# Tokens loaded with features on partitions, LayerNorm 1 applied behind the q product, low parts on GpSimd

## The reference

```
xn  = (x - mean(x)) / sqrt(var(x) + 1e-5)                 # LayerNorm 1
q   = head_norm(xn @ Wq + bq)                             # 16 heads of 32
k,v = split(y_main @ [Wk, Wv] + [bk, bv]); k = head_norm(k)
kd, vd = the same from y_dca @ Wkv_dca
x1  = x + (softmax(q k' s) v + softmax(q kd' s) vd) @ Wo + bo
out = x1 + fake_quant(relu(fake_quant(LN(x1)) @ fake_quant(F) + fake_quant(b)))
```

## Time and profile before

| | us |
|---|---|
| median of 3 runs | 370.63 |
| lowest, highest run | 370.16, 372.56 |
| profiled execution: span from the first to the last instruction | 366.4 |
| busy in the span: PE, DVE, ACT, POOL | 317.5, 315.4, 225.1, 173.5 |

### The profile page before, as it was taken

How to read it: one execution, slowest core, us unless ns; L and a number is a source line. 1 busy time by engine, 2 the same in 40 slices (tenths; PEclk the granted TensorE clock), 3 DMA queues, 4 the chain that set the end, 5 groups by cost and what they waited for, 6 DMA issues and landing times.

```text
span 366.4 us, 7583 instructions
## 1 busy us (share of the span) xinstructions
PE 317.5 (87%) x2338; PEld 255.8 (70%) x2353; DVE 315.4 (86%) x804; ACT 225.1 (61%) x444; POOL 173.5 (47%) x261
## 2 busy tenths in 40 slices
PE   1498987999999899999999999999999999868732
PEld 0355556788888778787878787878787887665620
DVE  3997989999888899999898989899989898875664
...
GB/s 268 267 266 1 88 161 130 93 98 95 81 112 73 148 68 154 62 160 56 165 31 190 30 191 34 189 23 195 19 202 5 155 24 160 18 144 2 29 0 86
DMA packets 36451, 39.14 MB, mean 107 GB/s; under 512 B 8760, under 2 KB 27452, under 8 KB 36412
## 3 DMA queue, kind: packets, MB, share of 16 engines
...
## 4 chain that ended last, share of the span: by engine, by line
PE 60%; DVE 13%; issue 8%; ACT 8%; DMA 4%; SPq 3%; POOL 3%; ACTq 1%; DVEq 0%; POOLq 0%
PE bank L1326 29%; PE bank L1443 10%; PE bank L1412 3%; SPq L372 3%; PE bank L1599 3%; PE bank L1423 2%; PE bank L1424 2%; PE bank L1609 2%; DMA q_stack<-q_lo 2%; POOL finals L530 2%; PE bank L1466 2%; PE bank L1501 2%; PE bank L1496 1%; DMA k_stack<-k_lo 1%; DVE head_mean L897 1%
## 5 line engine op out<-in xcount | busy, mean ns | idle before, releaser
L1443 PE MATMUL bank<-v_aug,prob_store 128*128 128x66 f32 x512 | 67.2, 274 | 2.4 <-ACT prob_store L744 2.1
L511 POOL TENSOR_TENSOR k_lo<-wkv_raw,k_hi 128x448 f16<-128x448 f32 x16 | 16.8, 1048 | 109.1 <-issue 101.2
L1443 PEld LDWEIGHTS bank<-v_aug,prob_store 128*128 128x128 f32 x512 | 63.1, 191 | 5.0 <-ACT prob_store L744 3.4
L1059 DVE TENSOR_REDUCE neg_max<-bank 128x4 f32<-128x448 f32 (+1 forms) x128 | 45.1, 414 | 6.4 <-PE bank L1412 6.3
L755 ACT ACTIVATE wkv_raw<-bank,affine 128x448 f32<-128x448 f32 (+1 forms) x32 | 22.5, 749 | 42.4 <-PE bank L1496 42.1
L744 ACT ACTIVATE prob_store<-bank,exp_scale 128x512 f32<-128x512 f32 x64 | 42.0, 683 | 7.5 <-PE bank L1424 6.4
L530 POOL TENSOR_TENSOR finals<-seg_out 128x128 f32<-128x128 f32 x64 | 34.5, 548 | 17.8 <-DVE seg_out L1072 17.5
L1423 PE MATMUL bank<-q_stack,k_stack 128*128 128x128 f16 x256 | 33.9, 220 | 1.4 <-ACT maxT L606 1.4
L1424 PE MATMUL bank<-maxT,sel 128*128 128x128 bf16 x256 | 33.7, 219 | 0.0
L1072 DVE TENSOR_TENSOR seg_out<-bank,rden 128x256 f32<-128x256 f32 x64 | 27.2, 424 | 3.8 <-POOL finals L530 1.7
L1423 PEld LDWEIGHTS bank<-q_stack,k_stack 128*128 128x128 f16 x256 | 26.4, 104 | 5.5 <-issue 3.8
...
## 6 DMA issues: line engine op xcount, KB each, us to landing
...
q_stack<-q_hi SPq DMA_DIRECT2D x32, 128.0 KB, 3.6
q_stack<-q_lo SPq DMA_DIRECT2D x32, 128.0 KB, 4.7
k_stack<-k_hi SPq DMA_DIRECT2D x32, 128.0 KB, 3.3
k_stack<-k_lo SPq DMA_DIRECT2D x32, 128.0 KB, 4.3
...
y_in<-in_ctx SPq DMA_DIRECT2D x16, 128.0 KB, 4.4
...
```

Source lines behind the costliest of these rows:

```text
L1059: v.tensor_reduce(neg_max[:, HG * gr:HG * (gr + 1), seg], s4[:, :, lo:hi], AX.X, ALU.max, negate=True).then_inc(max_ready.sem, 1)
L1443: last = mm(bank[6 + gr % 2][:, VW * h:VW * (h + 1)], probs[:, gr % 2, h], v_aug[:, Bt.parity, HG * gr + h], start=True, stop=True)
```

## The change

The host lays the tokens out once more, as `tokens_T` with features on partitions (x: 4 chunks of 128 tokens, y: 2 chunks of the 112 main tokens), and lays the six norm vectors and the value biases out as one row array and one column array.

- **Loads.** xyT (376 KB a batch) replaces y_in (128 KB). x_in is still loaded, for the statistics. In the start-up Wk and Wv are issued first; six norm loads and three bias loads become one each.
- **PE.** The transposes of y and x go. The transpose of the maxima moves behind the k product. In the start-up `setup_columns` goes and `setup_sums` comes: ones times Wq, in plain fp32, so that each column sum of Wq stands on all partitions.
- **LayerNorm 1.** The q product runs on raw tokens. With r = 1/std and s = -mean x r, q_raw = r x bank + (s x column sums + bias). The bracket, q_shift, is made by POOL (a scale and an add of 128x512), the rest by DVE as the product leaves PSUM.
- **High parts.** ACT copies them from SBUF instead of PSUM. q_hi now always comes before maxT.
- **Low parts.** POOL subtracts (low_context, low_stream), before k_lo in its order, and in step t = -1 behind the dca keys. DVE no longer does.
- **ACT in the start-up** rounds Wq, then waits for the column sums and copies them, and only then copies the biases.

```diff
-            def tokens(i):
-                sp.dma_start(y_in[:, i], ctx[i]).then_inc(y_loaded.sems[i], 16)
-                sp.dma_start(x_in[:, i], x[i]).then_inc(x_loaded.sems[i], 16)
-
-            tokens(0)
             for i in range(2):
                 load(wkv_in, wkv_raw[:, i], chunked((Wk, Wv)[i]))
+            load(first_context, context_in(0), xyT[0, :, D:D + YC * MAIN])
+            sp.dma_start(x_in[:, 0], x[0]).then_inc(x_loaded.sems[0], 16)
             load(wd_in, wd_raw[:].rearrange("p c s n -> p c (s n)"), chunked(Wkv_dca))
             load(wq_in, wq_raw[:], chunked(Wq))
-            tokens(1)
-            for n, w in enumerate((qn_w, qn_b, kn_w, kn_b, kn_dca_w, kn_dca_b)):
-                load(norms_in, norm_w[:, n], row(w))
-            for n, b in enumerate((bk, bv)):
-                load(bv_in, bv_rows[2 * n:2 * n + 2].rearrange("c (h d) -> c h d", d=HD),
-                     b.rearrange("(c h s d) -> c h s d", c=2, s=2, d=HD)[:, :, 1])
-            load(bv_in, bv_rows[4:8, :], bkv_dca[D:2 * D].rearrange("(c n) -> c n", n=P))
+            sp.dma_start(stream_in(0), xyT[0, :, 0:D]).then_inc(xy_loaded.sems[0], 16)
+            sp.dma_start(x_in[:, 1], x[1]).then_inc(x_loaded.sems[1], 16)
+            sp.dma_start(xy_in[:, 1], xyT[1]).then_inc(xy_loaded.sems[1], 16)
+            load(norms_in, norm_w[:].rearrange("p n d -> p (n d)"), row(norms))
+            load(cols_in, cols[:], columns)
 ...
-                    sp.wait_ge(*xn_ready.of(prev))
+                    sp.wait_ge(*ln1_steps.of(prev, 2))
                     sp.dma_start(x_in[:, L.parity], x[L.index()]).then_inc(x_loaded.sem(L), 16)
-                    sp.wait_ge(*yT_ready.of(prev))
-                    sp.dma_start(y_in[:, L.parity], ctx[L.index()]).then_inc(y_loaded.sem(L), 16)
+                    for read in (xhi_ready, xlo_ready, yhi_ready, ylo_ready):
+                        sp.wait_ge(*read.of(prev))
+                    sp.dma_start(xy_in[:, L.parity], xyT[L.index()]).then_inc(xy_loaded.sem(L), 16)
 ...
+                def low_tokens(lo, hi, src, loaded, hi_ready, used, done):
+                    pool.wait_ge(*loaded)
+                    pool.wait_ge(*hi_ready.of(A))
+                    if A.has(1):
+                        pool.wait_ge(*used.of(A.back(1)))
+                    g.tensor_tensor(lo[:].rearrange("p c n -> p (c n)"), src,
+                                    hi[:].bitcast(FP32).rearrange("p c n -> p (c n)"), ALU.subtract
+                                    ).then_inc(done.sem, 1)
+
+                def low_context():
+                    loaded = (first_context.sem, 16) if A.first() else xy_loaded.of(A)
+                    low_tokens(yT_lo, yT_hi, context_in(A.parity), loaded, yhi_ready, v_ready, ylo_ready)
+
+                def low_stream():
+                    low_tokens(xT_lo, xT_hi, stream_in(A.parity), xy_loaded.of(A), xhi_ready, q_ready, xlo_ready)
+
+                def query_shift():
+                    if A.first():
+                        pool.wait_ge(wqsum_copied.sem, 1)
+                        pool.wait_ge(bias_copied.sem, 2)
+                    pool.wait_ge(*ln1_shift.of(A))
+                    if A.has(1):
+                        pool.wait_ge(*qraw_ready.of(A.back(1)))
+                    g.tensor_scalar(q_shift[:], wq_sum[:], x_shift[:, A.parity:A.parity + 1], None, ALU.mult
+                                    ).then_inc(qshift_scaled.sem, 1)
+                    pool.wait_ge(*qshift_scaled.of(A))
+                    g.tensor_tensor(q_shift[:], q_shift[:], bias_full[:, 0], ALU.add).then_inc(qshift_ready.sem, 1)
+
                 if A is not None and A.first():
+                    low_context()
                     low_values()
-                    setup_rows()
+                    low_stream()
+                    query_shift()
                 if D is not None and not final(D):
 ...
                         dca_columns(k_hi, kdca_hi)
                         dca_columns(k_lo, kdca_lo)
-                        low(k_lo, k_n, k_hi, kn_ready, khi_ready, kstack_in, klo_ready, MAIN)
+                if A is not None and not A.first():
+                    low_context()
+                    low_stream()
+                    query_shift()
+                if N is not None and not N.first():
+                    low(k_lo, k_n, k_hi, kn_ready, khi_ready, kstack_in, klo_ready, MAIN)
                 centred()
 ...
                     pool.wait_ge(*ln1_steps.of(L))
-                    g.tensor_tensor(x_small[:, 2:3], x_small[:, 1:2], minus_half[:], ALU.pow
+                    if L.has(2):
+                        pool.wait_ge(*qraw_ready.of(L.back(2)))
+                    g.tensor_tensor(x_rstd[:, p:p + 1], x_small[:, 1:2], minus_half[:], ALU.pow
                                     ).then_inc(ln1_rstd.sem, 1)
+                    pool.wait_ge(*ln1_rstd.of(L))
                     if L.has(2):
-                        pool.wait_ge(*xT_ready.of(L.back(2)))
-                    pool.wait_ge(*ln1_rstd.of(L))
-                    g.tensor_scalar(x_norm[:, p], x_in[:, p], x_small[:, 0:1], x_small[:, 2:3], ALU.add, ALU.mult
-                                    ).then_inc(xn_ready.sem, 1)
+                        pool.wait_ge(*qshift_ready.of(L.back(2)))
+                    g.tensor_tensor(x_shift[:, p:p + 1], x_small[:, 0:1], x_rstd[:, p:p + 1], ALU.mult
+                                    ).then_inc(ln1_shift.sem, 1)
 ...
-            def setup_weights():
+            def setup_weights(high_stream):
                 for n in range(2):
                     act.wait_ge(wkv_in.sem, 16 * 2)
                     copy(value_half(wv_hi[:], n), value_heads(n)).then_inc(wvhi_ready.sem, 1)
                 setup_transposed()
+                high_stream()
                 for half in range(2):
                     act.wait_ge(wq_centred.sem, half + 1)
                     part = slice(XC // 2 * half, XC // 2 * (half + 1))
                     copy(wq_hi[:, part], wq_raw[:, part]).then_inc(wqhi_ready.sem, 1)
+                act.wait_ge(wqsum_ready.sem, 1)
+                copy(wq_sum[:], bank[0][:, :]).then_inc(wqsum_copied.sem, 1)
 ...
-                    act.wait_ge(*yT_ready.of(A))
-                    if A.has(1):
+                    if A.first():
+                        act.wait_ge(first_context.sem, 16)
+                    else:
+                        act.wait_ge(*xy_loaded.of(A))
                         act.wait_ge(*v_ready.of(A.back(1)))
-                    copy(flat(yT_hi[:]), bank[1][:, 0:CD]).then_inc(yhi_ready.sem, 1)
-                    act.wait_ge(*xT_ready.of(A))
-                    if A.has(1):
-                        act.wait_ge(*q_ready.of(A.back(1)))
-                    copy(flat(xT_hi[:]), bank[0][:, :]).then_inc(xhi_ready.sem, 1)
+                    copy(flat(yT_hi[:]), context_in(A.parity)).then_inc(yhi_ready.sem, 1)
+
+                    def high_stream():
+                        act.wait_ge(*xy_loaded.of(A))
+                        if A.has(1):
+                            act.wait_ge(*q_ready.of(A.back(1)))
+                        copy(flat(xT_hi[:]), stream_in(A.parity)).then_inc(xhi_ready.sem, 1)
+
                     if A.first():
                         setup_keys()
-                        setup_weights()
+                        setup_weights(high_stream)
+                    else:
+                        high_stream()
 ...
                     high(k_hi, k_n, kn_ready, MAIN, kstack_in, khi_ready)
-                if Bt is not None and Bt.first():
                     high(q_hi, q_n, qn_ready, P, qstack_in, qhi_ready)
                 if Bt is not None:
                     act.wait_ge(*maxP_ready.of(Bt))
                     if Bt.has(1):
                         act.wait_ge(*shifted_ready.of(Bt.back(1)))
                     copy(maxT[:], bank[1][:, :].bitcast(BF16)[:, 0:P]).then_inc(maxT_ready.sem, 1)
-                if N is not None and not (Bt is not None and Bt.first()):
-                    high(q_hi, q_n, qn_ready, P, qstack_in, qhi_ready)
-                    if N.first():
-                        setup_columns_left()
+                if N is not None and N.first():
+                    setup_columns_left()
 ...
                 def biased_queries():
                     dve.wait_ge(*q_ready.of(A))
-                    if A.first():
-                        dve.wait_ge(bias_copied.sem, 2)
                     if A.has(2):
                         dve.wait_ge(*qt_ready.of(A.back(2)))
                         dve.wait_ge(*qsq_ready.of(A.back(2)))
-                    v.tensor_tensor(q_raw[:, A.parity], bank[2][:, :], bias_full[:, 0], ALU.add
-                                    ).then_inc(qraw_ready.sem, 1)
+                    dve.wait_ge(*qshift_ready.of(A))
+                    dve.wait_ge(*ln1_rstd.of(A))
+                    v.scalar_tensor_tensor(q_raw[:, A.parity], bank[2][:, :], x_rstd[:, A.parity:A.parity + 1], q_shift[:],
```

(43 more changed lines are left out.)

99 lines of the change are left out of this document (51 added, 48 removed).

## The result

| | before | after |
|---|---|---|
| time, median of 4 runs | 371.60 us | 406.36 us |
| spread | 370.16 to 372.78 | 403.61 to 407.90 |
| span of the profiled execution | 366.4 | 403.1 (time 404.88) |
| mean granted TensorE clock of it | 0.977 | 0.895 |

After over before is 1.0955, with a 95% interval of 1.0904 to 1.1006: slower by 9.5%. The forecast was 373.2 us with a range of 366.5 to 381.5. (Now and then an execution is over 1.5% slower than the fastest of the same kernel; such ones are left out of the ratios and intervals, not of the medians.)

What follows compares the result with a forecast made beforehand. PE and DVE were nearly full, SP and transfers also setting the step's second stretch; DVE would become the bound. Span 366.4 + 7.8 start-up - 5.2 steady + 4.2 median over span gave 373.2 us, range 366.5 to 381.5.

Steps and rivals of the forecast that it cites:

- The ceiling of the steady gain, 0.6 us a step from the transposes: PE, first stretch of a step: removing six transposes saves at most 0.6 of 0.66 us, 7.8 us over 13 steps.
- VectorE's round of 18.1, mean 18.4: VectorE's steady step: 18.1 us with port stalls, mean 18.4 with slow issues; 0.4 less a step, 5.2 us in all.
- k_lo behind it ends at 10.1 instead of 9.8: GpSimd's steady step: k_lo, behind q_shift's add, ends at 10.1 us after the first scores instead of 9.8.
- The maxima: PE's steady step: moving the maxima's transpose behind the k product saves only a short wait the transfers cover; gain nothing.
- Start-up, +9.4, net +7.8, bounds 4 and 10: Start-up: two in-order queues made to wait cost 9.4 us, net +7.8 after the next step; bounds 4 and 10.
- (1): Start-up, PE and ACT: ACT's queue waits for setup_sums, so the square of q ends at 34.8, +4.4 us.
- (2): Start-up, POOL: second batch's low parts stand behind first-batch key work; q_raw comes at 48.0, +5.0 us.
- taken back in the next step: Step after the start-up: 0.9 us regained for transposes and 0.7 of PE's 1.01 us wait for the maxima.
- A: Rival, steady step: the shared port does no harm, steps take 18.15 us against 18.77; 370.3 us, chance 0.20.
- B: Rival, steady step: POOL's add gets the port before max_parts, which waits 1.2 us; 381.6 us, chance 0.17.
- C: Rival, start-up: its waits meet unseen slack and cost less than 4 us; 366.4 us, chance 0.12.
- D: Rival, transfers: the larger token load holds up q_lo by 0.3 us a step; 377 us, chance 0.09.

Runs made afterwards that it cites:

- keys_first: The changed kernel with VectorE taking k_raw ahead of the maximum over f_cent instead of behind it: 378.50 us, 1.017 of before.
- before_keys_late: The kernel before with k_raw moved one place back in VectorE's order, behind the first seg_out: 384.96 us, 1.029 of before.
- shift_last: The changed kernel with q_shift computed at the end of GpSimd's step before instead of ahead of k_lo: 378.48 us, 1.016 of before.
- maxima_ahead: shift_last with the maxima's transpose ahead of the k product on TensorE again: 400.82 us.
- mended versions: Changed kernel with q_shift ending GpSimd's step, key squares behind the third exponential, start-up edits: 375.09 us; with low parts on VectorE: 380.04 us.
- before_loads: The kernel before with 256 KB more loaded in each step by the same number of issues, read by nothing: 372.35 us, 1.001 of before.

## Why the prediction was wrong, step by step

- **The ceiling of the steady gain, 0.6 us a step from the transposes, and VectorE's round of 18.1, mean 18.4.** Near in size once the link is cut, but in part by luck. keys_first has 18.47, 0.30 less than before where I gave 0.4. Of the 0.6 only 0.24 came: the output product starts 3.28 us behind the first scores (mean of ten steps) where it was 3.52. PE now waits ahead of it for GpSimd's last combination of the weighted values (finals L528, 3.3 us in ten steps; 0.7 before), and cT_lo is later for it. VectorE's stalls are 1.7 us a step where I had 1.2, and other ones: none at q_t (I gave 0.55), 0.69 at cast and max_parts (0.40), 0.17 at q_lo (0.26), and 0.85 at L1267, which I had left out.
- **"k_lo behind it ends at 10.1 instead of 9.8."** Mis-sized: 11.7 (233.31 - 221.64). Three terms add up. yT_lo ends at 6.05 and not at 4.85: GpSimd did not get between k_t and q_t but waited for both (its 0.66 us took 2.31). That makes 0.4 behind the stream's low part (7.3 for 6.9), since there I had q_t in front anyway. The scale, 0.77 by x_norm's row, takes 1.57, and so in every one of its 16 instances, 1562 to 1579 ns, also in the second batch's, which has no VectorE instruction beside it; that is its price and no stall. And k_lo itself takes 1.49, beside q_lo, where I left it at 1.04.
- **What the sum left out, the step that failed.** I made the steady sum as a round of VectorE's durations, and asked of k_lo only when its transfer is issued. I did not ask what is queued on GpSimd behind k_lo: the power and f_cent, then on VectorE L1286 with k_raw behind it, then on ScalarE the squares with expo(2) behind them, then weigh(2). The power, k_raw and expo(2) are late by their place in an order, not by their data; what lies between them waits for one of them. f_cent ends 13.3 us behind the first scores where it was 11.6, k_raw starts at 14.4 where it was 12.6, and the period is 20.5. before_keys_late shows the link in the old kernel (13 us), keys_first shows its whole price in the new one (27.9 us). The mis-size and the missing path were both needed: shift_last takes q_shift out of the way of k_lo and keys_first cuts the path, and either ends the steady loss.
- **The clock** had no place in the sum: I took PE's times at 1.00 throughout. PE's longer busy time is two thirds of the steady loss (14.1 of 21.2 us in ten steps).
- **The maxima: "nothing".** Right in the sum, as the move is in the changed kernel, wrong as a price: undone in shift_last, it costs 22 us (maxima_ahead).
- **Start-up, +9.4, net +7.8, bounds 4 and 10.** Measured +9.7 at the first scores. (1) came out: the square of q was forecast at 34.8 and starts at 34.78. In (2) q_raw of the second batch was forecast at 48.0 and came at 54.39, since I laid its queue on old times, though (1) had moved k_hi by 4.8 us already, and left out that the stream's low part and q_shift stand behind y's low part on GpSimd and in front of q_raw. The first scores don't wait for all of that, so the sum held partly by luck. The 1.6 us "taken back in the next step" were not: the next step grew by 2.5.
- **Rivals.** A (370.3, the port does no harm): its time is what the mended versions reach, for another reason; the stalls are there. B (the add ahead of max_parts): no, max_parts takes 0.64 and not 1.2. C: no. D: no, by before_loads, and q_lo lands in 4.1 us (median) in after where it was 4.7; xyT lands in 4.1, not 1 us later than y_in's 4.4. None was "a wait that GpSimd's lateness passes on", the one that the rows of ScalarE ahead of k_sq (17.0 us in all before) would have told of.
- **The signs that I named.** VectorE's idle time ahead of rden did not go (9.9 us in all, 6.8 before), and the period of 20.5 is outside all branches. Of q_t and cast only the cast grew (0.18 to 0.43); k_t and q_t held the port. The cast reads one SBUF tensor, so that two inputs from SBUF are not the whole condition here, as I had it. The first scores came some 9 us later and GpSimd's idle time ahead of k_lo went, as the forecast had it; neither tells it from what happened.

The Trainium skill (SBUF — State Buffer, Who interferes with whom) has it that whoever issues first blocks the other for its whole instruction. The traces agree in both directions: yT_lo alone takes 0.66 us and 2.31 beside k_t and q_t, and L1267 0.68 alone and 1.53 beside k_lo. My sum, which priced the stalls by that rule, had the step at 18.4 and not at 20.5.
